# Mean-embedding projection: a tile's last 14 gathers are added onto the first twelve's buffers by the DMA, masks go, tiles join later

## What is computed

```python
valid    = sequence_ids < 12500                     # (1024 users, 200), about one id in nine is valid
seq_emb  = emb_table[where(valid, ids, 0)] * valid  # rows of 512 floats
user_repr = seq_emb.sum(axis=1) / max(valid.sum(axis=1), 1)
logits   = user_repr @ proj_w + proj_b              # (1024, 512) @ (512, 12500)
```

## Time and profile before

| what | us |
|---|---|
| median of 3 runs (642.55 to 642.87) | 642.86 |
| the profiled execution's own time | 643.35 |
| its span, first to last instruction | 641.6 |
| PE busy | 609.1 |
| DVE busy | 407.9 |
| POOL busy | 233.6, all of it in the first 340 us |
| ACT busy | 137.6 |

### The profile page before, as it was taken

How to read it: one execution, slowest core, us unless ns; L and a number is a source line. 1 busy time by engine, 2 the same in 40 slices (tenths; PEclk the granted TensorE clock), 3 DMA queues, 4 the chain that set the end, 5 groups by cost and what they waited for, 6 DMA issues and landing times.

```text
span 641.6 us, 7583 instructions
## 1 busy us (share of the span) xinstructions
PE 609.1 (95%) x2602; PEld 476.1 (74%) x2602; DVE 407.9 (64%) x723; ACT 137.6 (21%) x153; POOL 233.6 (36%) x227
## 2 busy tenths in 40 slices
PE   1878799989999999999999999999999999999997
PEld 0326558777778787788788788888888888888886
DVE  7977958989878898697786454333333333344442
ACT  7605426132122131300200221110011111211210
POOL 5777777777764767566550000000000000000000
PEclk9999989999999999999999999999999999999999
DMA  9979999999998999798793398454555555566632
GB/s 311 388 259 331 380 390 293 373 329 318 315 296 298 305 291 313 236 323 249 236 341 121 97 288 260 127 173 161 177 176 177 176 177 176 171 185 201 223 127 103
DMA packets 77703, 158.31 MB, mean 247 GB/s; under 512 B 9287, under 2 KB 65042, under 8 KB 77658
## 3 DMA queue, kind: packets, MB, share of 16 engines
q1 hardware_dynamic: 60378, 110.30, 50.7%
q0 software_dynamic: 17280, 47.47, 23.2%
HBM read 115.70 MB, written 51.20 MB: 260 GB/s over the span
## 4 chain that ended last, share of the span: by engine, by line
PE 75%; DVE 13%; DMA 6%; issue 5%; ACT 1%; DVEq 1%; POOL 0%; POOLq 0%; ACTq 0%
PE acc L801 70%; DVE sums L539 5%; DMA rows<-in_L_rec_emb_table_dram,index 4%; PE turned L757 2%; DMA w_raw<-in_L_rec_proj_w_dram 2%; DVE w_lo L597 2%; DVE key L496 1%; DVE w_lo L595 1%; DVE top L492 1%; PE acc L806 1%; ACT w_hi L416 1%; DVE stage L609 1%; PE turned L749 1%; DVE mean L584 0%; PE turned L732 0%
## 5 line engine op out<-in xcount | busy, mean ns | idle before, releaser
L347 POOL DMA_INDIRECT rows<-in_L_rec_emb_table_dram,index x208 | 224.1, 1077 | 95.7 <-issue 58.1
L801 PE MATMUL acc<-w_hi,mean_hi 128*128 128x500 f32 x800 | 224.4, 402 | 0.8 <-ACT mean_hi L422 0.8
L609 DVE TENSOR_TENSOR stage<-acc,bias_sb 128x500 f32<-128x500 f32 x162 | 109.3, 676 | 179.4 <-PE acc L801 179.3
L801 PE MATMUL acc<-w_hi,mean_lo 128*128 128x500 f32 x800 | 213.8, 389 | 0.3 <-DVE mean_lo L589 0.3
L801 PE MATMUL acc<-w_lo,mean_hi 128*128 128x500 f32 x800 | 214.0, 389 | 0.0
L801 PEld LDWEIGHTS acc<-w_hi,mean_lo 128*128 128x128 f32 x800 | 150.1, 188 | 32.4 <-DVE mean_lo L589 1.6
L801 PEld LDWEIGHTS acc<-w_hi,mean_hi 128*128 128x128 f32 x800 | 150.2, 189 | 31.9 <-issue 4.3
L801 PEld LDWEIGHTS acc<-w_lo,mean_hi 128*128 128x128 f32 x800 | 150.2, 188 | 31.3
L539 DVE SCALAR_TENSOR_TENSOR sums<-rows,mask,sums 128x512 f32<-128x512 f32 x165 | 124.1, 752 | 8.8 <-DMA rows<-in_L_rec_emb_table_dram,index 0.6
L416 ACT ACTIVATE w_hi<-w_raw 128x2000 fp32r<-128x2000 f32 x39 | 72.9, 1875 | 236.3 <-PE acc L801 215.7
L595 DVE TENSOR_TENSOR w_lo<-w_raw,w_hi 128x1000 fp32r<-128x1000 f32 x39 | 46.5, 1193 | 13.4 <-ACT w_hi L416 13.3
(11 more groups left out here) (106 smaller groups left out, 180.9 us busy)
## 6 DMA issues: line engine op xcount, KB each, us to landing
out_dram<-stage SPq DMA_DIRECT2D x200, 250.0 KB, 3.8
w_raw<-in_L_rec_proj_w_dram SPq DMA_DIRECT2D x39, 1000.0 KB, 6.6
bias_sb<-in_L_rec_proj_b_dram SPq DMA_DIRECT2D x39, 250.0 KB, 4.9
raw_at_hi<-in_L_rec_proj_w_dram SPq DMA_DIRECT2D x4, 1000.0 KB, 11.1
rows<-in_L_rec_emb_table_dram,index POOLq DMA_INDIRECT x208, 5.8
raw_at_lo<-in_L_rec_proj_w_dram SPq DMA_DIRECT2D x3, 1000.0 KB, 13.7
stage<-in_L_rec_proj_w_dram SPq DMA_DIRECT2D x1, 1000.0 KB, 23.8
ids_sb<-in_r_sequence_ids_dram SPq DMA_DIRECT2D x1, 700.0 KB, 4.4
```

Source lines behind the costliest of these rows:

```text
L347: return pool.indirect_dma_start(out=dst, out_offset=None, in_=table, in_offset=bass.IndirectOffsetOnAxis(ap=column, axis=0), bounds_check ...
L609: dve.tensor_tensor(stage[:, g % STAGE, r - stores[g][0]], acc[:, r % BANKS, 0:BW], bias_sb[:, i % BIAS], ALU.add).then_inc(s_moved_by_dve, 1)
L801: last = nc.tensor.matmul(bank, first, second, start=part + k == 0, stop=part == 2 and k == K - 1 and not by_act[r])
```

## The change

Columns 12 to 25 of a tile are now gathered with an add: the DMA adds the fetched row to what the buffer holds. Columns 0 to 11 overwrite, 12 to 23 add onto them, 24 and 25 add onto the buffers of 12 and 13. So 12 buffers hold the sum of 26 columns, and only these 12 (the *closing* columns, j = 14 to 25) are added up by an engine: by PE for tile 0 (with the plain identity as weights), by DVE for tiles 1 to 7. The adding gather waits for the landing of the earlier gather into its buffer. The table gets one more row, of zeros, at index 12500, so that an invalid place fetches zeros and is not skipped; masks, diagonals and the clearing of buffers go. Tiles join at loads 13, 17, 20, 22, 24, 26, 28: `joined` becomes 0, 13, 25, 38, 50, 64, 79, 95, and the loads 49. `BOTH_TILES` becomes 3, so 25 units are moved out by ACT.

```diff
-                              JOIN=(0, 10, 14, 17, 20, 22, 24, 26)):
+                              JOIN=(0, 13, 17, 20, 22, 24, 26, 28)):
-    ITEMS, HID = table.shape
+    ROWS_HELD, HID = table.shape
+    ITEMS = ROWS_HELD - 1
...
-    ON_PE, DIAGS = ((0, FAST), (18, FAST), (24, FAST)), 4
+    CLOSING, PE_TILES = FAST - ROWS, 1
-    ACT_TILES, BOTH_TILES = 1, 5
+    ACT_TILES, BOTH_TILES = 1, 3
...
+    closing = [c for c in range(COLS) if c % FAST >= CLOSING]
+    by_pe = [c < FAST * PE_TILES for c in range(COLS)]
+    nth = [sum(by_pe[x] == by_pe[c] for x in closing if x < c) for c in range(COLS)]
+    GATHER_LEAD, FIRST_DUE = 5, 2
...
-        if by_pe[c]:
-            return joined[t] - 2
-        begin, end = joined[t - 1] - 2 if t > 1 else 0, joined[t] - SUM_AHEAD
-        return begin + (end - begin) * j // (dve_last[t] - FAST * t)
+        begin, end = joined[t - 1] - 2 if t > 1 else FIRST_DUE, joined[t] - SUM_AHEAD
+        return begin + (end - begin) * j // (FAST - 1)
...
-                    bounds_check=ITEMS - 1, oob_is_err=False)
+                    bounds_check=ITEMS, oob_is_err=False)
+            def gather_onto(dst, column):
+                return pool.indirect_dma_start(
+                    out=dst, out_offset=None, in_=table,
+                    in_offset=bass.IndirectOffsetOnAxis(ap=column, axis=0),
+                    bounds_check=ITEMS, oob_is_err=True, compute_op=ALU.add)
...
-                    if c % CH == 0:
-                        if c < ROWS:
-                            pool.wait_ge(s_zeroed, c // CH + 1)
-                        else:
-                            wait_used(pool, c - ROWS + CH - 1)
-                        if t > 1 and column_due(c) > GATHER_LEAD:
-                            wait_moved(pool, column_due(c) - GATHER_LEAD - 1)
+                    if j >= ROWS:
+                        pool.wait_ge(s_rows[c % ROWS], 16 * (c // ROWS))
+                    elif t:
+                        wait_used(pool, c - ROWS)
+                    if t > 1 and column_due(c) > GATHER_LEAD:
+                        wait_moved(pool, column_due(c) - GATHER_LEAD - 1)
...
-                    gather(rows[:, c % ROWS], index[:, t, j:j + 1]).then_inc(s_rows[c % ROWS], 16)
+                    (gather_onto if j >= ROWS else gather)(rows[:, c % ROWS], index[:, t, j:j + 1]).then_inc(
+                        s_rows[c % ROWS], 16)
...
-            for g in range(ROWS // CH):
-                clear(g)
...
-                if j == 0:
+                if j == CLOSING:
...
-                    dve.scalar_tensor_tensor(sums[:], rows[:, c % ROWS], mask[:, t, j:j + 1], sums[:], ALU.mult,
-                                             ALU.add).then_inc(s_summed, 1)
+                    dve.tensor_tensor(sums[:], rows[:, c % ROWS], sums[:], ALU.add).then_inc(s_summed, 1)
...
-                pe.wait_ge(s_diag, nth[c] + 1)
-                nc.tensor.matmul(turned[:], diagonal_of(c), rows[:, c % ROWS], start=j == 0,
+                nc.tensor.matmul(turned[:], ident[:], rows[:, c % ROWS], start=j == CLOSING,
...
-            for c in pe_columns[0]:
+            for c in closing[0:ROWS]:
...
+        if name == "L0_rec_emb_table":
+            a = _np.concatenate([a, _np.zeros((1, a.shape[1]), a.dtype)])
```

More of the change, by code:

```diff
@@ L171, in mean_embedding_projection @@
         w_raw = sb("w_raw", [P, RAW, K, BW], F32)
-        with ExitStack() as over_halves:
-            last_halves = []
-            for part in ("hi", "lo"):
-                over_halves.enter_context(nc.sbuf_tensor(f"before_diags_{part}", [P, SPLIT - 1, K, BW], F32))
-                last_halves.append(over_halves.enter_context(nc.sbuf_tensor(f"diags_at_{part}", [P, K * BW], F32)))
         w_hi = sb("w_hi", [P, SPLIT, K, BW], F32R)
@@ L181, in mean_embedding_projection @@
         stage = sb("stage", [P, STAGE, GROUP, BW], F32)
-        slot_row = diag[:, 0].bitcast(I32)
-        first_diags = [half[:, P * i:P * (i + 1)] for half in last_halves for i in range(K * BW // P)]
         start_area = stage[:].rearrange("p g m n -> p (g m n)")
@@ L389, in _ @@
         def _(act):
-            def clear(g):
-                nc.scalar.activation(rows[:, CH * g:CH * (g + 1)].rearrange("p c d -> p (c d)"),
-                                     zero[:, 0:1].to_broadcast([P, CH * HID]), ACT.Copy).then_inc(s_zeroed, 1)
-            def diagonal(c):
-                if nth[c] >= len(pe_columns[0]) + DIAGS:
-                    act.wait_ge(s_added, nth[c] - DIAGS + 1)
-                t, j = divmod(c, FAST)
-                nc.scalar.activation(diagonal_of(c), ident[:], ACT.Copy, scale=mask[:, t, j:j + 1]).then_inc(s_diag, 1)
             def move_out(r):
@@ L429, in rest_share @@
             def rest_share(t):
-                if t < len(ON_PE):
-                    act.wait_ge(s_added, sum(len(x) for x in pe_columns[0:t + 1]))
                 act.wait_ge(s_rest, t + 1)
@@ L446, in _ @@
             nc.scalar.activation(bias_parts[:], bias_raw, ACT.Copy).then_inc(s_bias_hi, 1)
-            for c in pe_columns[0][8:]:
-                diagonal(c)
             place(0)
@@ L459, in _ @@
                 for t in range(1, TILES):
-                    if r + (2 if t < len(ON_PE) else REST_AHEAD) == joined[t]:
+                    if r + REST_AHEAD == joined[t]:
                         rest_share(t)
-                for c in range(FAST, COLS):
-                    if by_pe[c] and column_due(c) == r + 1:
-                        diagonal(c)
                 for q in range(SPLIT, LOADS):
@@ L693, in _ @@
             mean_low(0)
-            for c in range(FAST, FAST + 4):
-                add_column(c)
             fill_slots(1)
@@ L705, in _ @@
                         w_low(q)
-                for t in range(1, len(ON_PE)):
-                    if r + 2 == joined[t]:
-                        mean_of(t)
                 for c in range(FAST, COLS):
-                    if not by_pe[c] and column_due(c) == r and c >= FAST + 4:
-                        add_column(c)
+                    if column_due(c) == r:
                         t, j = divmod(c, FAST)
+                        if j >= CLOSING:
+                            add_column(c)
                         if 1 < t and t + 1 < TILES and j in SORT_NEXT:
@@ L778, in _ @@
                 for t in range(1, TILES):
-                    if r == (column_due(FAST * t + ON_PE[t][0]) if t < len(ON_PE) else joined[t] - REST_AHEAD):
+                    if r == joined[t] - REST_AHEAD:
                         sum_rest(t)
-                for c in range(FAST, COLS):
-                    if by_pe[c] and column_due(c) == r:
-                        sum_column(c)
                 if r + TURN_AHEAD in joined[1:]:
```

46 lines of the change are left out of this document (10 added, 36 removed).

## The result

| | us | to before |
|---|---|---|
| before, runs beside it | 642.7 | |
| after, median of 4 runs | 698.3 (698.0 to 699.8) | 1.087 [1.085, 1.089] |
| span of the profiled executions | 641.6 → 696.2 | +54.6 |

The forecast was 632; 698 lies outside its range and 12 above rival A.

A forecast was written before the change was run, and what follows sets the result against it. PE was taken as busy nearly throughout, its joins set by gathers, with POOL's issue and the DMA engines both near their limits early. Terms -9.9 - 1.0 - 2.9 - 1.5 + 4 = -11.3 from 643.35 gave 632 us, range 620 to 672.

The forecast's parts named there:

- rival A: At the adding gathers: adding costs the DMA engines twice, lengthening tiles 1 to 4 by about 13 each; 686 us, chance 0.22.
- The choice at the adding gathers: An adding gather was priced like a plain one on POOL and in the DMA engines: 0 us more.
- the gain is gone at 0.16 us each on either side: Over tiles 0 to 4, 70 adding gathers costing 0.16 us more each, on DMA or POOL, cancel the 11 us won.
- A's signs: L337 landings well over 8 us, PE waiting 10 or more at tile 1's join, first unit after 56.
- B: Rival at POOL's issue: an adding gather takes 1.3 us in place of 1.00; 650 us, chance 0.11; sign: L337 over 1.2.
- Tile 1, -9.9: At tile 1's later join: three more units done 1.1 us earlier, unit 12 starting near 91.9; -9.9 us.
- Wrong in size: Sign of a wrong size: waits at tiles 2 and 4 joins over 3 us each, or ACT waiting for weight blocks 9 to 12.
- PE's clock: PE's clock around tile 1's join, read at 0.95, was left unchanged because a wait of that size stays.
- Later joins, 0: Joins after tile 2: tightest 12 units, 35.7 us against 35.2 of gathers, no room but no loss; 0 us.
- DVE, bias: 25 bias matmuls instead of 38, -2.9 us; relief of DVE ending small waits at later joins, -1.5 us.
- Zero rows, +4: Gathers no longer skipping invalid rows need more DMA time over tiles 1 to 3; +4 us, bounds 0 and +8.
- Start, 0 (-2 to +8): Before the first unit: PE's 26 columns become 12, but the last gathers add; 0 us, bounds -2 and +8.

The follow-up runs named there:

- e1: The changed kernel with the last 14 gathers of each tile plain and overwriting, so sums hold 12 columns only; 652.3 us, 1.011.
- e3: The changed kernel with the adding gathers' bound at 0, so they are issued but skip nearly all rows; 669.9 us, 1.040.
- e5: e1 with bound 0 in the last 14 gathers of each tile, plain gathers that fetch nearly nothing; 632.0 us, 0.983.
- e9: The kernel before with only the change's table of joins and `BOTH_TILES` = 3; 659.0 us, 1.023.
- e6: e1 with DVE's adds and means ahead of the low weight splits, and tile 1's last adds, rest sum and mean two units sooner; 644.3 us, 1.003.
- e4: The kernel before with the row of zeros and its index in bounds, so invalid places fetch zeros; 645.2 us, 1.003.
- e2: The changed kernel with its adding gathers skipping invalid rows again, sums complete; 678.7 us, 1.057.
- e13: e1 with a memset of 128x690 on POOL behind each of the 112 gathers, giving the adding form's pace with plain transfers; 669.6 us, 1.043.

## Why the prediction was wrong

**The choice at the adding gathers.** The step that failed first is "I take the plain gather as the nearest row, so 0 more". Neither unknown was near it. On POOL: 1.549 us, the middle of 1.00 to 2.00. In the DMA engines: e1's plain gathers take 24.9% of 651.6 us, 162.2 over 216, 0.751 each; in the changed kernel 236.7 less 104 of those leaves 158.6 for 112, **1.42** each (an estimate, since it takes the plain ones at e1's price), 1.9 times as much, near the upper bound of one gather more. The packet records of the trace agree: the adding gathers' 14336 packets of 2 KB take 182 ns each, so 128 of them 1.46 us of 16 engines, where the plain ones beside them pack two rows into one packet, 6656 of 4 KB at 172 ns. Together the two cost 46 us. The remark that the gain is gone at 0.16 us each on either side was right as a warning: the costs were 0.55 and 0.67. The argument against A was that the new traffic is not HBM's and that 384 GB/s had been moved. The windows refute it: the share is 1.03 at 285 GB/s. What is full is the engines' time, well under the highest rate.

The Trainium skill ("Collectives: The Full Stack", the bandwidth ceiling, on ReduceScatter) states of ReduceScatter that its add needs two source reads, both through one ring, and so gives half the rate of AllGather, with a measured ratio of 1.93. For the gathers here this trace agrees in the engines' time, 1.42 against 0.75 us; the packets of an adding gather are 144 against 80 (7168 more over 112).

Rival A, which priced this, had a chance of 0.22 and the forecast 0.57: with no row of an adding DMA, A was under-weighted. Its 686 would still have been 12 short, since it had nothing for POOL.

**Rival A's number, with both mechanisms.** A's signs came: landings of L337 at 9.0, 14 us of wait at tile 1's join, first unit at 60.8, 9 later where A said 6. But two of the three don't tell A from B: e3, where the adding gathers move nothing, has 14.5 us of wait there and the first unit at 56.5. B's sign came too: 1.55, where B had reckoned with 1.3. B's own sum with 0.55 in place of 0.3, 14 x 0.55 x 5 = 38, is what e5 to e3 cost. Each was priced alone and they were taken as alternatives. The case of both at once had no price. That A's number is only 12 off is in part luck: A started from 628, and the kernel without the add took 652.

**Tile 1, -9.9.** This is the second step that failed, and by itself, as e1 shows: unit 12 starts there at 104.6, not near 91.9. The step took the last gather as the last thing to come, and said of the weight blocks "That just fits". They did not: in e9 ACT waits for blocks with the gathers of before, PE behind it, and the joins with `BOTH_TILES` cost 15 us. Missing in the working was what stands *between* in DVE's and ACT's programs. The mean was put behind three splits whose blocks come late, so a late block held up the mean, which had nothing to do with it; undoing that gave back 5 to 8 us (e6; by the interval 1 to 10). What was named as "Wrong in size" (ACT waiting for weight blocks 9 to 12) came in the changed kernel too. ACT's timeline, then DVE's:

```profile
98.32 1.87 ACT L389 ACTIVATE w_hi<-raw_at_hi 128x2000 fp32r<-128x2000 f32 x1 [7.25 <-DMA raw_at_hi<-in_L_rec_proj_w_dram]
...
107.16 1.87 ACT L389 ACTIVATE w_hi<-raw_at_lo 128x2000 fp32r<-128x2000 f32 x1 [6.50 <-DMA raw_at_lo<-in_L_rec_proj_w_dram]
```
```profile
100.22 1.20 DVE L553 TENSOR_TENSOR w_lo<-raw_at_hi,w_hi 128x1000 fp32r<-128x1000 f32 x1 [5.30 <-ACT w_hi L389]
...
109.06 1.20 DVE L553 TENSOR_TENSOR w_lo<-raw_at_lo,w_hi 128x1000 fp32r<-128x1000 f32 x1 [4.33 <-ACT w_hi L389]
...
116.14 3.09 DVE L498 TENSOR_TENSOR sums<-rows,sums 128x512 f32<-128x512 f32 x4
120.53 0.75 DVE L542 SCALAR_TENSOR_TENSOR mean<-sums,inv_count,rest_mean 128x512 f32<-128x512 f32 x1 [1.30 <-issue]
```

Tile 1's last gather is issued at 96.65, so it has landed by about 106 (9.0 for the landing), and its mean starts at 120.5: what ends last at this join is the weight block in front of the adds, not the rows.

**PE's clock.** It was left as it is, since a wait like that of the earlier trace rows stays. The waits were longer, and the granted clock, a mean over stretches at its two levels (1.2 and 2.4 GHz), fell over 51 to 200 from 0.99 to 0.87. Instructions of the same kind take longer behind the waits: first product matmuls of a unit 2.04 for four against 1.24, the turns 1.11 against 0.66. So a wait cost more than its own length. An estimate of how much: PE runs the same 2541 matmuls in e1 and in the changed kernel and is busy 591.8 and 600.5 us, so some 9 of the 46 us between them are a slower PE.

**Later joins, 0.** In e1 they lose 9.4 us between units 12 and 50 and then nothing (the table). "No room, but no loss" was too kind: e9 shows 13.7 over the same units, and 6.8 of it between 37 and 50, where tile 4 now joins after 12 units and no longer after 16. The 35.2 us for a tile's gathers that the step took was their least; "today's pace", which the prediction has in its second paragraph, was 38 to 40 a tile, already more than the 35.7 us of 12 units.

**DVE, bias.** The work went as forecast: 25 bias matmuls, DVE 52 us less busy. The relief of DVE was to end the small waits at the means; in e1 PE's waits for means are 19.6 in all against 3.9 before, so it bought nothing that shows there. In the step from e9 to e1, where the ten PE columns, diagonals and half of DVE's adds go and the zero rows come, some 7 us are given back; which of them gives it was not tried apart.

**Zero rows, +4.** Measured +2 (e4), within the bounds. In the changed kernel the zero rows of the adding gathers cost 19.6 (e2), for 8.4 MB (56.64 against 48.29). In time of the 16 DMA engines that is 32.5 us, against 17.8 for the 9.2 MB of e4, so the doubled price is there, but it alone would make 2 into 4. The rest must lie in what else differs between the two kernels, the joins and POOL's pace among it; no run tells.

**Start, 0 (-2 to +8).** e1: +0.6. In the changed kernel +9.3: 14 gathers at 0.55 more are 7.7 on POOL, of which e13 shows 5.6 net, and 3.1 come with the add in the DMA engines. The upper bound had covered only one of the two.

## What to carry to other kernels

Before an edit that leaves work to the DMA, cost both of its resources for each transfer, the issuing engine's time and the DMA engines' time, and price the case of both together; a share that read 0.9 to 1.0, as here, had no room for the second, whatever the GB/s were. Where a join or a result is moved later, list everything that stands ahead of it in the in-order programs of the engines that make it: it waits for the latest input of any of them, not only for its own. And one run with the plain operation in the place of the new one divides "the new operation" from "the new order" at once.

## What was not expected of the hardware

- An adding indirect gather of 128 rows holds POOL for 1.549 us against 0.999, also when all its rows are skipped (1.548). It makes 144 packets against 80, takes about 1.42 us of all 16 DMA engines against 0.75, and lands in 9.0 us against 6.9 for plain ones beside it.
- What skipping rows saves is not in proportion to their bytes: 9.2 MB of zeros cost 2 us in the kernel before, with plain gathers (e4), 8.4 MB cost 19.6 us in the changed one, with adding gathers (e2), and taking away 20.9 MB more brought only 8.9 (e3).
- After a wait of PE the granted clock was low: 0.59 in the window 100 to 120, in which PE was busy 4.8 of 20 us, so most of it lies at the lower of the clock's two levels. The window of the changed kernel:

```profile
100.00:120.00 20.00, 4.79 (x13) 3.49 (x13) 13.62 (x16) 6.88 (x9) 9.66 (x9) 0.59 1.05 370
```

- Left open: the doubled time in the DMA engines without POOL's longer issue, which needs an adding transfer that POOL issues at the plain pace; and why POOL's pace costs 7 us at 1.70, 17 at 1.85 and 38 at 1.85 with nothing fetched for the last 14 columns. e6's order of DVE's program was tried with plain gathers only.
